# Moving a router's normalisation and top-4 selection to other slots of an attention loop, its square root to another engine, and two experts' weight loads to the head of their queue

## Reference

```python
def _L0_attn_ref(x, w_qkv, scale, w_out, b_out):     # 16 heads of 8 channels
    ...
    allow = jnp.tril(jnp.ones((n, n), dtype=bool), k=-1)
    attn = _masked_softmax(dots, allow)
    out = jnp.einsum('bhnm,bhmd->bhnd', attn, v)
    return out @ w_out + b_out

def _L0_ffn_ref(hidden_states, router_w, router_b, w1, b1, w2, b2):   # 16 experts, top 4
    logits = hidden_states @ router_w + router_b
    probs = jax.nn.softmax(logits, axis=-1)
    topw, topi = jax.lax.top_k(probs, K)
    topw = topw / jnp.sum(topw, axis=-1, keepdims=True)
    combine = jnp.sum(jax.nn.one_hot(topi, E, dtype=...) * topw[..., None], axis=2)
    ...   # every expert on every token, weighted by combine
        hmid = jax.nn.gelu(x @ w1e + b1e, approximate=False)
        acc + (hmid @ w2e + b2e) * ce[:, None]

x = x + _L0_attn_ref(_layernorm(x, axis=-1), ...)
x = x + _L0_ffn_ref(_layernorm(x, axis=-1), ...)
x = x + _L1_attn_ref(_layernorm(x, axis=-1), ...)
x = x + _L1_ffn_ref(_layernorm(x, axis=-1), ...)
```

## Time and profile before

| | |
|---|---|
| median of 3 runs | 1085.29 us (1080.76 to 1086.73) |
| the profiled execution | 1087.06 us, its span on the chip 1085.0 us |
| mean granted TensorE clock | 0.918 of 2.4 GHz |
| busy share of the span: PE, DVE, ACT, POOL | 86%, 70%, 59%, 48% |
| attention0 (16.0 to 282.7 us) | 266.7 us, clock 0.87 |
| experts0 (282.7 to 485 us) | 202.3 us, clock 0.96 |

### The profile page before, as it was taken

The page is one execution under the profiler, slowest core; times in us unless marked ns, Lnnn a source line. Parts: engine busy times, 40 slices in busy tenths (PEclk is TensorE's granted clock), DMA queues, the critical chain, the costliest instruction groups (busy, mean ns, idle before and its releaser), DMA issues. The chain is left out here.

```text
span 1085.0 us, 18688 instructions
## 1 busy us (share of the span) xinstructions
PE 930.7 (86%) x5892; PEld 604.4 (56%) x5892; DVE 760.8 (70%) x2133; ACT 636.0 (59%) x1372; POOL 525.8 (48%) x614
## 2 busy tenths in 40 slices
PE   2999898988869999986899899999999977950796
PEld 1444344443546888864556566656665644650585
DVE  4577676773567999987889798889888887352121
ACT  1366666564556888873567657765776566720353
POOL 4043324231214444401366867686768678915155
PEclk9999798995689999997999999999999989965798
DMA  6000000000068455510000000000000000006630
GB/s 186 1 1 1 1 2 21 2 22 1 21 144 214 115 122 120 116 20 1 1 1 2 1 1 2 2 1 2 2 1 2 2 1 1 2 0 223 201 119 14
DMA packets 32246, 45.84 MB, mean 42 GB/s; under 512 B 3644, under 2 KB 20305, under 8 KB 32160
## 3 DMA queue, kind: packets, MB, share of 16 engines
q1 hardware_dynamic: 30000, 41.57, 14.7%
q0 software_dynamic: 1728, 3.17, 0.8%
q10 hardware_dynamic: 432, 0.01, 0.0%
HBM read 37.48 MB, written 8.17 MB: 42 GB/s over the span
## 5 line engine op out<-in xcount | busy, mean ns | idle before, releaser
L1385 POOL TENSOR_SCALAR probs<-probs,rinv 128x128 f32<-128x128 f32 (+3 forms) x256 | 273.8, 1084 | 115.4 <-DVE rinv L1258 115.4
L1320 ACT ACTIVATE probs<-probs,rowmin 128x128 f32<-128x128 f32 (+3 forms) x256 | 141.6, 558 | 41.2 <-DVE rowmin L1252 40.1
L1329 ACT ACTIVATE pt<-psum 128x128 f32<-128x128 f32 (+3 forms) x256 | 98.1, 434 | 97.9 <-PE psum L1125 96.6
L1252 DVE CUSTOM_DVE_ANT_0 probs<-psum,adj 128x128 f32<-128x128 f32 (+3 forms) x256 | 122.1, 477 | 40.7 <-PE psum L1115 25.2
L751 ACT ACTIVATE pT<-psum 128x1024 f32<-128x1024 f32 (+3 forms) x128 | 89.8, 702 | 76.2 <-PE psum L546 75.2
L1115 PE MATMUL psum<-k_sb,q_sb 64*128 64x256 f32 (+3 forms) x512 | 110.7, 485 | 23.9 <-DVE rowmin L1252 23.2
L682 DVE TENSOR_REDUCE top<-psum 128x2 f32<-128x256 f32 (+3 forms) x128 | 103.0, 818 | 26.2 <-PE psum L534 26.0
L1640 ACT ACTIVATE m_hid<-psum,b1t 128x512 f32<-128x512 f32 x128 | 85.0, 689 | 39.0 <-PE psum L1496 38.7
L1241 DVE MAX8 top<-w 128x8 f32<-128x131 f32 (+3 forms) x208 | 103.2, 496 | 4.6
L1583 DVE TENSOR_TENSOR m_hid<-m_hid,r_share 128x1024 f32<-128x1024 f32 x64 | 85.6, 1338 | 28.1 <-ACT m_hid L1640 17.9
L808 POOL TENSOR_SCALAR_AFFINE_SELECT pT<-pT 128x512 f32<-128x512 f32 x64 | 40.7, 636 | 130.4 <-ACT pT L751 129.9
(11 more groups left out here) (271 smaller groups left out, 1886.8 us busy)
## 6 DMA issues: line engine op xcount, KB each, us to landing
r_share<-shares SPq DMA_DIRECT2D x14, 1024.0 KB, 8.6
s_wb<-in_w_all SPq DMA_DIRECT2D x15, 514.5 KB
sorted_x<-blank SPq DMA_DIRECT2D x1, 3870.0 KB, 26.8
s_xg<-sorted_x SPq DMA_DIRECT2D x15, 258.0 KB, 6.0
r_w1s<-in_w SPq DMA_DIRECT2D x16, 128.0 KB, 7.7
r_w2s<-in_w SPq DMA_DIRECT2D x16, 128.0 KB, 8.0
r_share<-shares SPq DMA_DIRECT2D x8, 256.0 KB, 3.6
x_tok<-in_x SPq DMA_DIRECT2D x4, 256.0 KB, 4.0
```

The costliest lines, as they stand in the source:

```text
L1252: dve.tensor_tensor_reduce(probs[:, k, 0:K], s_bank[h][:, 0:K], adj[:, OFF[i]:OFF[i] + K], 1.0, FLOOR, ALU.add, ALU.min, rowmin[:, k:k + 1 ...
L1320: act.activation(probs[:, k, 0:K], probs[:, k, 0:K], ACT.Exp, bias=rowmin[:, k:k + 1], scale=-1.0, accum_out=rsum[:, k:k + 1]).then_inc(ex ...
L1329: act.activation(pt[:, (2 * n + h) % 4, 0:K], t_bank[h][:, 0:K], ACT.Copy).then_inc(pt_ready, 1)
L1385: pool.tensor_scalar(probs[:, k, 0:K], probs[:, k, 0:K], rinv[:, k:k + 1], None, ALU.mult).then_inc(normed, 1)
```

## The change

In `attention0` the pieces of the router move to other slots, four fills of `fills_at` with them; the square root of the variance of batches 0 to 2 is left out on ACT and is formed on POOL, as a power of -0.5 with two Newton steps (`pool_root`); POOL also writes `r_xn` (`pool_norm`). In `experts0` the four weight loads of experts 2 and 3 go to the head of SP's queue; the last chunk's shift, exponential, selection and `ct` (`pe_comb_last` and its copy) are written earlier in the programs of DVE, ACT and PE.

```diff
@@ class Routing
+            def pool_root(self, pool, q):
+
+                _, ts = self.tiles(q)
+                v, y, z = self.ve[:, ts], self.rs[:, ts], self.sd[:, ts]
+                pool.wait_ge(self.var_ready, q + 1)
+                n = q * 9
+                if q == 0:
+                    pool.memset(self.power[:], -0.5).then_inc(self.root_step, 1)
+                    pool.wait_ge(self.root_step, 1)
+                n += 1
+                pool.tensor_tensor(y, v, self.power[:], ALU.pow).then_inc(self.root_step, 1)
+                for k in range(2):
+                    pool.wait_ge(self.root_step, n + 4 * k + 1)
+                    pool.tensor_tensor(z, y, y, ALU.mult).then_inc(self.root_step, 1)
+                    pool.wait_ge(self.root_step, n + 4 * k + 2)
+                    pool.tensor_tensor(z, z, v, ALU.mult).then_inc(self.root_step, 1)
+                    pool.wait_ge(self.root_step, n + 4 * k + 3)
+                    pool.tensor_scalar(z, z, -0.5, 1.5, ALU.mult, ALU.add).then_inc(self.root_step, 1)
+                    pool.wait_ge(self.root_step, n + 4 * k + 4)
+                    pool.tensor_tensor(y, y, z, ALU.mult).then_inc(self.root_step, 1)
+
+            def pool_norm(self, pool, q):
+                tiles, ts = self.tiles(q)
+                pool.wait_ge(self.root_step, (q + 1) * 9 + 1)
+                for i, t in enumerate(tiles):
+                    ins = pool.tensor_scalar(self.xn[:, i, :], x_tok[:, t, :], self.mv[:, t, 0:1], self.rs[:, t:t + 1],
+                                             ALU.subtract, ALU.mult)
+                ins.then_inc(self.xn_ready, 1)
...
@@ fills_at
-                if p == 9 and u == 3 and 1 <= b < B:
-                    out.append(("xr", b - 1))
-                if p == 5 and u == 0 and 2 <= b <= B:
+                if p == 1 and u == 0 and 2 <= b <= B:
+                    out.append(("xr", b - 2))
+                if p == 9 and u == 0 and 2 <= b <= B:
                     out.append(("lg", b - 2))
-                if p == 13 and u == 1 and 2 <= b <= B:
+                if p == 5 and u == 2 and 2 <= b <= B:
                     out.append(("ct", b - 2))
@@ dve_route (slot l: stats 44 -> 48, aggr 50, norm 48 -> gone, split 60 -> 4 and 6, shift 8 -> 16,
@@            largest 14 -> 20, taken 16 -> 32, chosen 18 -> 34, shares 20 -> 36)
                     if 1 <= b < B:
-                        if l == 44:
+                        if l == 48:
                             R.dve_stats(dve, b - 1)
...
+                        if l == 50:
+                            R.dve_aggr(dve, b - 1)
@@ act_program
-                        if 1 <= b < B and l == 46:
-                            R.act_root(act, b - 1)
-                        if 2 <= b <= B and l == 10:
+                        if 2 <= b <= B and l == 18:
                             R.act_exp(act, b - 2)
@@ pool_program (attention0), r counts clears, four slots each
+                        b, k = divmod(r, UNITS * NT)
+                        if 1 <= b < B and k == 6:
+                            R.pool_root(pool, b - 1)
+                        if 1 <= b < B and k == 7:
+                            if b >= 2:
+                                pool.wait_ge(filled, fill_no["xr", b - 2] + 1)
+                            R.pool_norm(pool, b - 1)
@@ experts0: pe_pair, dve_pair, dve_program
-                        if isinstance(t, int) and t == 0 and m == 3:
+                        if isinstance(t, int) and t == 0 and m == 1:
                             pe_comb_last(pe)
...
                             if m == 0:
-                                R.dve_shift(dve, LAST)
-                            if m == 1:
                                 R.dve_largest(dve, LAST)
                                 R.dve_taken(dve, LAST)
-                            if m == 2:
                                 R.dve_chosen(dve, LAST)
                                 R.dve_shares(dve, LAST)
...
-                    dve_low(dve, 0, 0)
                     dve.wait_ge(logits, 1)
                     R.dve_logits(dve, LAST, o_bank[LAST]).then_inc(biased, 1)
                     dve.wait_ge(biased, 1)
+                    R.dve_shift(dve, LAST)
+                    dve_low(dve, 0, 0)
@@ experts0: act_pair, act_program
-                            if m == 0:
-                                R.act_exp(act, LAST)
-                            if m == 3:
+                            if m == 2:
                                 act.wait_ge(comb_turned, 1)
...
                     act_hidden(act, 0, 1)
+                    R.act_exp(act, LAST)
                     act_round(act, 0, 0)
@@ experts0: sp_program (sp_later cut into sp_weights and sp_share)
+                    for u in range(2):
+                        sp_weights(sp, 0, u)
                     sp.dma_start(b2_e[:], a["b2_0"]).then_inc(comb_back, 16)
...
                     for u in range(2):
-                        sp_later(sp, 0, u, DONE[u])
+                        sp_share(sp, 0, u, DONE[u])
```

More of the change, by code:

```diff
@@ L203, in __init__ @@
                 self.rs = sbt("rs", [P, T])
+                self.power = sbt("power", [P, NT])
                 self.xn = sbt("xn", [P, NT, C])
@@ L266, in dve_norm, with dve_high, dve_low @@
                 ins.then_inc(self.xn_ready, 1)
-            def dve_split(self, dve, q):
+            def dve_high(self, dve, q):
                 cols = slice(q * N, (q + 1) * N)
                 dve.tensor_copy(self.xt_hi[:, cols], self.xt[:]).then_inc(self.xt_split, 1)
+            def dve_low(self, dve, q):
+                cols = slice(q * N, (q + 1) * N)
                 dve.wait_ge(self.xt_split, 2 * q + 1)
@@ L652, in dve_route @@
                     if 1 <= b < B:
[L653 removed]
+                        if l == 48:
                             R.dve_stats(dve, b - 1)
[L655 to L663 removed]
+                        if l == 50:
+                            R.dve_aggr(dve, b - 1)
+                    if 2 <= b <= B:
+                        if l == 4:
+                            dve.wait_ge(f_act, act_no["xr", b - 2])
+                            R.dve_high(dve, b - 2)
+                        if l == 6:
+                            R.dve_low(dve, b - 2)
+                        if l == 16:
                             dve.wait_ge(f_dve, dve_no["lg", b - 2])
                             R.dve_shift(dve, b - 2)
[L666 removed]
+                        if l == 20:
                             R.dve_largest(dve, b - 2)
[L668 removed]
+                        if l == 32:
                             R.dve_taken(dve, b - 2)
[L670 removed]
+                        if l == 34:
                             R.dve_chosen(dve, b - 2)
[L672 removed]
+                        if l == 36:
                             R.dve_shares(dve, b - 2)
@@ L1698, in pool_program, with sp_weights @@
                             pool_split(pool, e, u, t, (e - 1) * CH)
-                def sp_later(sp, t, u, done):
+                def sp_weights(sp, t, u):
                     e = bass.ds(t * 2 + 2 + u, 1)
@@ L1704, in sp_later, with sp_share @@
                     sp.dma_start(R.w2s[:, u, :, :], w2d[e].rearrange("e (f p) c -> p (e f) c", p=P)).then_inc(R.weights[u], 16)
+                def sp_share(sp, t, u, done):
+                    e = bass.ds(t * 2 + 2 + u, 1)
                     sp.wait_ge(scaled, done)
@@ L1718, in sp_program @@
                         for u in range(2):
-                            sp_later(sp, t, u, (t * 2 + u + 1) * CH)
+                            sp_weights(sp, t, u)
+                            sp_share(sp, t, u, (t * 2 + u + 1) * CH)
                 with nc.Block() as block:
```

21 lines of the change are left out of this document (7 added, 14 removed).

## The result

The changed kernel takes 1072.75 us (median of 14 runs, 1068.39 to 1082.65) against 1085.3 us (14 runs of the kernel before beside it, 1080.76 to 1093.54). The ratio is 0.9896, with a 95% interval of 0.9866 to 0.9925: about 11.3 us faster, between 8.1 and 14.5. Its profiled execution took 1073.11 us (span 1071.4), the one before 1087.06 (1085.0).

A forecast was written before the change was run, and what follows sets the result against it. PE, ACT and DVE stand in turn at the router's square root and PE's clock falls. Attention 10.5 + 4.7 - 1.1 = 14.1 us plus experts 1 gives 15 us: from the median of 1085.29 to 1070.3, range 1062 to 1082.

The forecast's parts named there:

- Attention, batches 2 and 3: attention0's second and third batches: 54.5 us each at 2.4 GHz against 59.65 and 59.88, 10.5 us gained.
- 13.66 - 0.7 = 13.0: Slots 9 to 25 of a batch: moving `taken`, `chosen` and `shares` out gains 0.7 us.
- The power: Root on POOL: power priced as a small operation, 0.29 us, upper bound 5 us; under 0.5 us would show the forecast right.
- rival 2: Root on POOL: power is slow; at 5 us each batch loses 4.7 us, clock stays low, 1095 us; chance 0.08.
- the square root's three-engine stand: attention0's root: PE, ACT and DVE stand in turn, clock goes from 2.4 to 1.2 GHz in each of three batches.
- Rival 1: attention0: clock falls anyway, only the direct stall is won, 4 us in all, so 1081 us; chance 0.17.
- Fourth batch and drain: attention0's end: 2.2 us for slots 41 to 57, 1.5 us for eight slots behind, 1.0 us in the drain.
- clock 1.00 until the fourth batch's scores end: Sign of being right in attention0: PE keeps the high clock until the fourth batch's scores end; no size given.
- Rival 4: attention0's drain: PE keeps 2.4 GHz through most of it, some 5 us less, 1064 us; chance 0.07.
- Tail: End of attention0's drain: `out` waits for the last `taken` to `shares` and for `ct`, -1.1 us.
- Experts: experts0 opening: PE's 8.09 us weight wait goes, third expert's share is late next; +1 us, between -3 and +3.
- that caps the gain near 2 us: experts0: `sorted_x`, 3.87 MB in 26.8 us, holds back the fifth expert's weights, limiting the gain near 2 us.

The follow-up runs named there:

- e4: Changed kernel with six Newton steps instead of two in the root on POOL; 1089.06 us, ratio 1.0027 to the kernel before.
- e5: Kernel before with ACT's square root made a plain copy in batches 1 to 3 of attention0, so no table loads there; 1084.56 us, ratio 0.9994.
- e9: Kernel before with statistics and aggregation moved to slot 48, root and r_xn following on their old engines, fills unmoved; 1082.11 us, ratio 0.9964.
- e10: Changed kernel with r_xn back on DVE (slot 56), root still on POOL; 1074.06 us, ratio 0.9899 to the kernel before.
- e1: Kernel before with only the attention0 change, old experts0; 1077.81 us, ratio 0.9911.
- e2: Kernel before with only the experts0 change, old attention0; 1081.27 us, ratio 0.9956.
- e8: Changed kernel, but in experts0 only the four weight loads moved, last chunk's pieces in old places; one execution, no ratio, experts0 197.88 us.
- e12: Changed kernel with the sorted_x load behind the fifth and sixth experts' loads; one execution, no ratio, experts0 209.96 us.
- e3: Changed kernel with the root back on ACT (slot 52) and r_xn back on DVE (slot 54); 1078.34 us, ratio 0.9924 to the kernel before.

## Why the prediction was right, and where not

The sum gave 1070.3, in 1062 to 1082, and 1072.75 came. The gain was 15 us in the sum and is 11.3 by the ratio (8.1 to 14.5), a quarter less. That the two spans differ by 13.6 us is partly luck: 2.3 of these us lie outside the two changed parts, and this profile of the changed kernel is one without a fall in batches 2 and 3. By its terms:

- *Attention, batches 2 and 3.* 54.5 us forecast, 55.19 and 55.01 measured; 10.5 us of gain forecast, 9.3 measured. Three quarters came out within 0.2 us (14.2, 13.4 and 13.9 against 14.41 and 14.21, 13.35 and 13.36, 13.76). The term that failed is l 9 to 25, "13.66 - 0.7 = 13.0": it measured 13.67. The step behind it is "`lg` stays in the same quarter". It doesn't: in the kernel before, `lg` lies in the quarter l 57 to 9 (128.17 to 143.94 us), in the changed one it opens l 9 to 25 (from 136.65 us). Timelines, before and after:

```profile
139.63 1.06 PE L506 MATMUL psum<-rw,r_xt 128*128 128x16 f32 x8
```

```profile
136.67 1.06 PE L543 MATMUL psum<-rw,r_xt 128*128 128x16 f32 x8 [0.67 <-DVE q L655]
```

  The sum starts the one quarter from a clean row without `lg` and the other from a row that never had it, so these 1.06 us are in neither. PE was idle for 1.56 us of 13.66 in l 9 to 25 before and is for 0.53 of 13.67 now: so it seems that `lg` filled what the moved selection freed.
- *The power.* "At the price of a small one", 0.29 us; it takes 1.05, within the bounds but not under the 0.5 us that was to show the forecast right. The late clears cost PE 0.89 and 1.10 us against 0.4 and 0.8. The quarters came out right all the same, so it seems that the 0.2 and 0.4 us charged for the aggregation and the halves were not there. `e4` bears out the slope of rival 2: 4.7 us lost by the times for 4.5 us more of root, where it had 4.7 for 5. A PE wait on the clears was listed as a sign of being wrong, though the sum itself charged 1.2 us a batch for it.
- *Why the clock falls.* The prediction blamed the square root's three-engine stand of the earlier trace rows and took the removal of the ACT block and of `r_xn` as the cure. `e5`, `e9` and `e10` show two separate stands: `yn` behind the statistics (1.75 us) and the exponential behind the table loads (1.67 us). Removing only one is worth nothing that can be measured (`e5`) or 3.9 us (`e9`), both together, with the moved fills, 9.7 us (`e1`). `r_xn` on DVE is no part of it (`e10`). The forecast held because the change removes both; the reason for moving the statistics was missed, since the rows read were those of the one batch without an `x` fill. That the change took away the stand for `yn` too was luck. What a stand must be for the clock to fall stays open: the same 1.75 us had no fall behind it in `e2`'s third batch, and 0.69 us had one in `e1`.
- *Direct or by the clock.* `e2`'s third batch against the changed kernel's shows 1.2 us won directly and 3.65 us by the clock. Rival 1 had 2.1 - 0.8 = 1.3 us a batch for the direct part, so it was right on that and wrong on the clock.
- *Fourth batch and drain.* 2.2 us forecast up to l 57, 2.14 measured. The 1.5 us behind it became 0.6, as the clock fell at the root after all: "clock 1.00 until the fourth batch's scores end" was wrong here. In `e1`, `e8` and `e12`, with the same `attention0`, that stretch took 14.26, 14.25 and 14.23 us instead of 16.89; there the clock came back to 2.4 GHz for some us in it. What decides it stays open. (Rival 4's own sum, 1070.3 less 5, gives 1065, not 1064.) The 1.0 us forecast for "part of the drain" didn't come: l 9 to 25 of the drain took 12.33 us against 11.13. From l 41 of the fourth batch to the last addition, 51.14 us against 51.84, 0.7 us were won where the sum has 4.7 - 1.1 = 3.6, the largest miss in the sum. But it hangs on the clock of the two executions: the same stretch takes 48.50 us in `e2` with the old code, and 46.64 to 48.06 in `e1`, `e8` and `e12`.
- *Tail.* -1.1 forecast. From the last `o` transposes to `out` it is 4.81 us (263.31 to 268.12) against 3.95 (275.95 to 279.90): -0.86. `ct` in front of `out` waits 0.92 us.
- *Experts.* +1 forecast, +1.25 measured between these two profiles and 0.65 between the means of all, by the mechanism told: the share is late next, the first second product is late too. But the sum hid two opposite terms, +3.0 for the loads and -1.76 for the pieces (`e8`). And "that caps the gain near 2 us", said of `sorted_x`, was wrong: nobody waits behind it in its old place (`e12`).

The Trainium skill (ScalarE: Activation LUTs, What ACT_TABLE_LOAD costs) has a drain of 1.38 us behind each load. In `e9` the root starts 1.30 us after its load began and the exponential 1.29 us after the second: no drain there either.

## To carry to other kernels

When engines walk in step and PE's clock falls, look for every stand within the stretch where it falls, in each repetition of it: two stands of equal length can hide each other, and the one that a view shows first may be worth nothing alone. Look at more than one profile of a kernel before pricing a fall, and before calling a stretch free of them. Price a bundled change by its parts once; here one of the moves was a loss inside a gain. A long transfer in an ordered queue costs by its place, so check what lies behind it at the old place and at the new one.

## What the hardware showed unexpectedly

- The same four `r_xn` operations on DVE take 1.11 us when POOL all but rests (`e3`, `e9`, `e10`) and 2.15 or 2.16 us in the kernel before, where three POOL operations of 0.63, 0.40 and 0.73 us run at the same moment (the clear and both halves of the weight cut). In `e5`, beside the last two only, they take 1.78 us. The Trainium skill (SBUF — State Buffer, Who interferes with whom) says that VectorE in some of its modes contends with GpSimd for a shared pair of ports, which one holds for a whole instruction while the other blocks. The traces agree in direction: DVE gets longer, POOL doesn't. But it gets longer by 1.05 and 0.67 us beside 1.76 and 1.12 us of POOL, about 0.6 of it, so that DVE is blocked for the whole of each POOL instruction isn't shown. The prediction's factor of 1.45 between POOL and DVE was taken from such a disturbed row: undisturbed it is 3.13 to 1.11, or 2.8, more also than the factor of two that it set beside it.
- A power of 128x4 elements on POOL takes 1.05 us, a product of the same size 0.20.
- The clock of one program differs from execution to execution. The old `attention0` fell in its third batch in one profile and not in another (`e2`), with 3.65 us between them; the changed one fell three times in `e1`'s second and third batches and not at all in these batches of its own profile. So single profiles of these kernels differ by several us for no change of the code.
